# The reciprocal of the WKV denominator moved from VectorE to POOL, as a power of -1, with the rounds put in a new order

## The chip, the cores and the metric

The kernel runs on one core of one Trainium2 chip. The metric is the device time of that core in microseconds. One further execution was profiled; its trace is what the rows below come from.

## What is computed

An audio tower over `x` of shape (64, 256, 192). Pairs of time steps are merged by a softmax (leaving 64 sequences of 128 tokens), then come an RWKV time mix, a GELU MLP, a 12-head attention with normalised q and k, and a mixture of eight experts of which each token uses two. The change is in the time mix, whose core is a recurrence per channel:

```python
def step(carry, kv):
    p, q, o = carry
    kt, vt = kv
    no = jnp.maximum(o, u + kt)
    A = jnp.exp(o - no)
    Bc = jnp.exp(u + kt - no)
    y = (A * p + Bc * vt) / (A * q + Bc)
    ...
return jnp.einsum('btc,oc->bto', sr * y, Wo)      # sr = sigmoid(r)
```

The kernel divides numerator and denominator by `A`, so that with `z = exp(u + k - o)` the value is `y = (p + z v) / (q + z)`: one denominator and one numerator for each channel and token.

## The kernel before

The 64 sequences are worked in 16 groups of four (512 tokens). Tower work is staged over rounds: in round i the engines hold group i+1 (`gn`), i (`ga`), i-1 (`gb`), i-2 (`gc`), i-3 (`gr`) and i-4 (`gs`) at different stages. Stage A is the merge and the time mix, B the GELU MLP, C the attention, R the router. Each of the five engines has a `round_` of its own in which the steps stand in an order written out by hand; every engine works through its list strictly in that order, and a step waits with semaphores for what others must have done. Rounds 5 to 14 are one hardware loop, the others are unrolled. The experts follow after the last round, in a second pipeline that the change leaves alone.

The time mix of a group on VectorE (DVE), in the order of its dependences, with channels on 96 partitions and 1024 columns (two halves of the channels times 512 tokens): `a_mix` prepares the inputs of the r, k and v projections; `a_exponents` scans the running maximum `o_s` (L1253); `a_fraction_args` makes the argument of z; `a_scan_p` and `a_scan_q` scan p and q (L1283, L1287); `a_denominator` adds z and q into buffer wkv1 (L1292); `a_reciprocal` inverts that in place, in four quarters of 256 columns (L1301); `a_numerator` makes z v + p in wkv3 (L1296, L1297); `a_gate` multiplies by the gate (L1309) and then by the reciprocal, which gives `sy` (L1311). PE projects `sy` in `a_project` (L475), and `a_residual` takes the result (L1316). ScalarE (ACT) does the exponentials, POOL the small work on layer-norm statistics: `rstd` raises a variance plus eps to the power of -0.5 with `tensor_tensor(..., ALU.pow)` against the constant tile `neg_half` (L1089), on 4 columns, or on 8 for q and k. POOL also issues the eight indirect DMAs of `r_scatter` (L1126).

Beside the WKV steps DVE serves the attention of another group: `c_max` (L1356) for the maxima that ACT's `c_exps` wait for, `c_values` (L1365, L1366) for the scaled values that PE's `c_values` waits for, and `c_attn_add` (L1379), which ends that group's attention and which PE's `a_project` waits for too (semaphore `hF_ready`), since both use the same PSUM banks.

Of the kernel before, what the change touches and what calls it, by code (L numbers as in the profile page):

```python
# [14 lines left out]
P = 128  # L15
# [30 lines left out]
def build_tower(nc, a, out):  # L46
# [29 lines left out]
    with ExitStack() as ctx:  # L76
# [20 lines left out]
        neg_half = sg("neg_half", [P, 2 * G])  # L97
        lane8 = sg("lane8", [P, G, E])
# [130 lines left out]
        def ring(depth, name, shape, dt=F32):  # L229
# [25 lines left out]
            keep_arg keep_ready take_arg take_ready z_ready zexp_ready sy_ready  # L255
# [197 lines left out]
        def _(pe):  # L453
# [215 lines left out]
            def round_(i):  # L669
                gn, ga, gb, gc, gr, _ = stages(i)  # L670
                if gb is not None: b_mlp_up(gb, (4,))
                if gb is not None: b_mlp_up(gb, (5,))
                if ga is not None: a_hidden(ga)
                if gb is not None: b_mlp_down(gb, (0,))
                if gc is not None: c_keys(gc, gr)
                if gb is not None: b_mlp_down(gb, (1,))
                if gb is not None: b_mlp_down(gb, (2,))
                if ga is not None: a_r(ga)
                if gc is not None: c_queries(gc, 0)
                if gb is not None: b_mlp_down(gb, (3,))  # L680
                if ga is not None: a_k(ga)
                if gc is not None: c_scores(gc, 0, 0)
                if gc is not None: c_scores(gc, 0, 1)
                if gc is not None: c_queries(gc, 1, gb)
                if ga is not None: a_v(ga)
                if gc is not None: c_scores(gc, 1, 0)
                if gc is not None: c_scores(gc, 1, 1)
                if gc is not None: c_queries(gc, 2, gb)
                if gc is not None: c_values(gc, 0, gb)
                if gc is not None: c_scores(gc, 2, 0)  # L690
                if gc is not None: c_scores(gc, 2, 1)
                if gc is not None: c_queries(gc, 3, gb)
                if gc is not None: c_values(gc, 1, gb)
                if gc is not None: c_scores(gc, 3, 0)
                if gc is not None: c_project(gc, 0, ga)
                if gc is not None: c_scores(gc, 3, 1)
                if gb is not None: c_transposes(gb)
                if gc is not None: c_project(gc, 1, ga)
                if gc is not None: c_values(gc, 2, gb)
                if gb is not None: c_qkv(gb, (0,))  # L700
                if gb is not None: c_qkv(gb, (1,))
                if gc is not None: c_project(gc, 2, ga)
                if gc is not None: c_values(gc, 3, gb)
                if gc is not None: c_project(gc, 3, ga)
                if gb is not None: c_qkv(gb, (2,))
                if ga is not None: a_project(ga, gc)
                if gb is not None: c_qkv(gb, (3,))
                if gn is not None: a_delta(gn)
                if gc is not None: r_transposes(gc, gb)
                if gn is not None: a_scores(gn)  # L710
                if ga is not None: b_transposes(ga)
                if gc is not None: r_logits(gc)
                if ga is not None: b_mlp_up(ga, (0,))
                if ga is not None: b_mlp_up(ga, (1,))
                if gc is not None: r_places(gc)
                if ga is not None: b_mlp_up(ga, (2,))
                if ga is not None: b_mlp_up(ga, (3,))
# [75 lines left out]
        def _(act):  # L793
# [127 lines left out]
            def round_(i):  # L921
                gn, ga, gb, gc, _, _ = stages(i)
                if gc is not None: c_queries(gc, 0)
                if ga is not None: a_kv(ga, "k", k_s)
                if gc is not None: c_exps(gc, 0, 0)
                if gc is not None: c_queries(gc, 1)
                if gc is not None: c_exps(gc, 0, 1)
                if ga is not None: a_kv(ga, "v", v_c)
                if ga is not None: a_take_exp(ga)
                if ga is not None: a_keep_exp(ga)  # L930
# [3 lines left out]
                if ga is not None: a_z_exp(ga)  # L934
                if gc is not None: c_exps(gc, 2, 0)
                if gc is not None: c_queries(gc, 3)
                if gc is not None: c_values(gc, 0)
                if gc is not None: c_exps(gc, 2, 1)
                if gb is not None: ln_out(gb, "c", hnC, hC, rstdC, shiftC)
                if gc is not None: c_values(gc, 1)  # L940
                if gc is not None: c_exps(gc, 3, 0)
                if gb is not None: transposed(gb, "c", hTC, 4)
                if gc is not None: c_exps(gc, 3, 1)
                if gc is not None: c_values(gc, 2)
                if gb is not None: c_qkv(gb, 0)
                if gc is not None: c_values(gc, 3)
# [7 lines left out]
                if gn is not None: a_scores(gn)  # L954
                if ga is not None: transposed(ga, "b", hTB, 2)
                if gb is not None: c_k_norm(gb)
                if ga is not None: b_gelu(ga, 0)
                if ga is not None: b_gelu(ga, 1)
                if gb is not None: c_q_norm(gb)
                if ga is not None: b_gelu(ga, 2)  # L960
                if gc is not None: r_twice(gc)
                if ga is not None: b_gelu(ga, 3)
                if gn is not None: ln_out(gn, "a", hnA, hA, rstdA, shiftA)
                if ga is not None: b_gelu(ga, 4)
                if ga is not None: b_gelu(ga, 5)
                if gc is not None: r_gap(gc)
                if gn is not None: a_hidden(gn)
                if gb is not None: c_residual(gb)
                if gn is not None: a_gate(gn)
# [81 lines left out]
        def _(pool):  # L1051
            init = Chain(pool, S["p_init"], 11)
# [12 lines left out]
            init.link(nc.gpsimd.memset(neg_half[:, :], -0.5))  # L1065
            init.link(nc.gpsimd.iota(lane8_i[:, :, :], [[0, G], [1, E]], base=0, channel_multiplier=0))
# [13 lines left out]
            def rstd(g, name, out_, shift_, mv, n):  # L1080
# [13 lines left out]
                last.then_inc(S[f"{name}_rstd"], 1)  # L1094

# [77 lines left out]
        def _(dve):  # L1173
# [29 lines left out]
            wkv = Chain(dve, S["d_wkv"], 9)  # L1203
# [85 lines left out]
            def a_denominator(g):  # L1289
                wkv.begin(g, 4)  # L1290
                dve.wait_ge(S["zexp_ready"], g + 1)
                wkv.link(nc.vector.tensor_tensor(keep_flat, z_s, q_s[:, 0:M], ALU.add))  # L1292

            def a_numerator(g):
                wkv.begin(g, 6)
# [3 lines left out]
            def a_reciprocal(g, n):  # L1299
# [145 lines left out]
            def round_(i):  # L1445
                gn, ga, gb, gc, gr, _ = stages(i)
                if gr is not None: c_values(gr, 2)
                if gb is not None: a_reciprocal(gb, 1)
# [190 lines left out]
```

## Time and profile before

| | |
|---|---|
| time, median of 3 runs | 2093.18 us (2091.97 to 2100.26) |
| the profiled execution's own time | 2086.18 us |
| its span, first to last instruction | 2084.4 us |
| instructions | 32990 |
| a_denominator of group 0 and of group 15 begin at | 69.5 us and 1269.9 us |
| mean granted clock of TensorE, as a share of 2.4 GHz | 0.874 |

The span covers all but 1.8 us of the profiled execution. The sixteen groups with a time mix fill about its first 1300 us; three rounds without one follow, and from about 1460 us on the experts run.

### The profile page before, as it was taken

The page shows a single profiled execution, that of the slowest core. Times are in us where ns is not written, and L with a number is a line of the kernel's source. Part 1 is how long each engine was busy: PE and PEld are TensorE (multiplying, and loading weights), DVE is VectorE, ACT ScalarE, POOL GpSimd, SP SyncE. Part 2 cuts the span into 40 slices and gives each one's busy share as a digit, 9 for nine tenths or more (in the row PEclk, how much of TensorE's full clock was granted, in tenths as well). Part 3 has the DMA queues.
Part 4 walks back from the last instruction along what each step waited for, and adds up shares of the span by engine and source line. Part 5 has one row for each costly group of instructions (what it writes and reads, how often), then busy time and mean ns, then how long its engine had stood idle before and what let it go on. Part 6 is the DMA issues. An engine that isn't in the chain of part 4 may idle for free.

```text
span 2084.4 us, 32990 instructions
## 1 busy us (share of the span) xinstructions
PE 1776.7 (85%) x10605; PEld 1384.4 (66%) x10605; DVE 1471.4 (71%) x2705; ACT 1230.0 (59%) x3205; POOL 737.6 (35%) x756
## 2 busy tenths in 40 slices
PE   2478989889889889899898897874799999999992
PEld 1345666657657567566666675553699999999992
DVE  3566686776876866866868758232698998999981
ACT  1236766765775676667657656552666666666660
POOL 0001122221321231231222213222377777767772
PEclk9789889889789899798898797765899999999996
DMA  3000000010010010010000100043676767667655
GB/s 80 12 4 16 23 22 29 24 37 23 28 36 23 28 36 23 24 34 28 21 25 26 36 8 29 22 149 103 176 177 150 181 154 171 165 161 177 148 118 141
DMA packets 119429, 149.49 MB, mean 72 GB/s; under 512 B 16948, under 2 KB 100007, under 8 KB 119271
## 3 DMA queue, kind: packets, MB, share of 16 engines
q1 hardware_dynamic: 86944, 114.23, 18.1%
q0 software_dynamic: 28608, 32.66, 8.9%
q10 hardware_dynamic: 3814, 1.83, 0.4%
q8 instruction: 33, 0.54, 0.1%
q14 instruction: 30, 0.24, 0.0%
HBM read 100.14 MB, written 54.83 MB: 74 GB/s over the span
## 4 chain that ended last, share of the span: by engine, by line
PE 69%; DVE 14%; ACT 6%; issue 5%; DMA 2%; POOL 2%; SPq 0%; ACTq 0%; POOLq 0%; DVEq 0%
PE ps L762 11%; PE ps L535 8%; PE ps L775 8%; PE ps L543 6%; PE ps L466 6%; PE ps L627 5%; PE ps L458 4%; PE ps L777 4%; PE ps L611 3%; DVE nmax L1356 3%; PE ps L475 3%; PE ps L559 3%; PE ps L638 2%; ACT probs L900 2%; DVE q_s L1287 2%
## 5 line engine op out<-in xcount | busy, mean ns | idle before, releaser
L1158 POOL DMA_INDIRECT total<-ey,etoken x156 | 275.6, 1767 | 156.7 <-DMA total<-ey,etoken 65.3
L900 ACT ACTIVATE probs<-ps,nmax 128x128 f32<-128x128 f32 x768 | 271.6, 387 | 49.3 <-DVE nmax L1356 49.2
L775 PE MATMUL ps<-w_hl,h_hi 128*128 128x384 f32 x936 | 274.6, 364 | 3.8 <-DVE ey L1578 3.8
L1035 ACT ACTIVATE h_full<-ps,eb 128x512 f32<-128x512 f32 x234 | 167.7, 717 | 162.8 <-PE ps L762 162.7
L777 PE MATMUL ps<-w_hl,h_lo 128*128 128x192 f32 x936 | 235.6, 252 | 0.0
L627 PE MATMUL ps<-probs,vpad 128*32 128x128 f32 x1536 | 105.6, 377 | 100.0 <-DVE vpad L1366 94.7
L777 PEld LDWEIGHTS ps<-w_hl,h_lo 128*128 128x128 f32 x936 | 180.5, 193 | 0.0
L775 PEld LDWEIGHTS ps<-w_hl,h_hi 128*128 128x128 f32 x936 | 177.4, 190 | 4.5 <-issue 4.4
L535 PE MATMUL ps<-hTB,w_up 96*128 96x512 f32 x384 | 175.4, 609 | 2.5 <-ACT hTB L877 2.2
L900 ACT ACTIVATION_READ_ACCUMULATOR probs<-ps,nmax 128x1 f32 x768 | 174.1, 227 | 0.0
L1148 POOL TENSOR_TENSOR w_lo<-w_raw,w_hi 128x1536 fp32r<-128x1536 f32 x39 | 157.6, 4042 | 36.3 <-ACT w_hi L1016 36.3
L1036 ACT ACTIVATE h_hi<-ps,eb 128x512 fp32r<-128x512 f32 x234 | 169.1, 722 | 0.0
L611 PEld LDWEIGHTS ps<-qT,kT 32*128 32x128 f32 x1536 | 121.3, 262 | 69.7 <-ACT probs L900 31.5
L1087 POOL TENSOR_SCALAR shiftR<-mvR 128x4 f32<-128x4 f32 x16 | 3.7, 232 | 457.7 <-DVE mvR L1215 457.7
L611 PE MATMUL ps<-qT,kT 32*128 32x128 f32 x1536 | 144.9, 374 | 23.5 <-ACT probs L900 16.2
L1356 DVE TENSOR_REDUCE nmax<-ps 128x6 f32<-128x768 f32 x128 | 120.5, 953 | 58.7 <-PE ps L611 55.3
L1126 POOL DMA_INDIRECT expert_rows_in<-rowR,slot_i x128 | 145.1, 1134 | 43.5 <-issue 41.5
L627 PEld LDWEIGHTS ps<-probs,vpad 128*32 128x32 f32 x1536 | 75.2, 148 | 126.4 <-DVE vpad L1366 104.5
L1539 DVE TENSOR_TENSOR h_lo<-h_full,h_hi 128x512 fp32r<-128x512 f32 x234 | 147.9, 686 | 15.4 <-ACT h_hi L1036 14.8
L762 PE MATMUL ps<-x_hl,w_hi 128*128 128x512 f32 x468 | 146.7, 395 | 5.5 <-DVE x_hl L1546 5.5
L762 PE MATMUL ps<-x_hl,w_lo 128*128 128x512 f32 x468 | 145.1, 391 | 0.0
L543 PE MATMUL ps<-w_down,hid 128*128 128x192 f32 x768 | 134.2, 328 | 0.8 <-ACT hid L881 0.8
(227 smaller groups left out, 3945.4 us busy)
## 6 DMA issues: line engine op xcount, KB each, us to landing
w_raw<-in_L_ffn_w SPq DMA_DIRECT2D x39, 576.0 KB, 4.7
ex<-expert_rows_in SPq DMA_DIRECT2D x39, 528.0 KB, 5.1
w_raw<-in_L_ffn_w SPq DMA_DIRECT2D x39, 384.0 KB, 5.4
w_raw<-in_L_ffn_w SPq DMA_DIRECT2D x78, 192.0 KB, 5.7
xt<-in_x SPq DMA_DIRECT2D x16, 768.0 KB, 4.5
expert_rows_in<-xt SPq DMA_DIRECT2D x17, 528.0 KB, 7.4
total<-resC SPq DMA_DIRECT2D x16, 384.0 KB, 2.6
eb<-in_L_ffn_b SPq DMA_DIRECT2D x39, 96.0 KB, 3.6
```

What stands on the lines that cost most here:

```text
L535: last = nc.tensor.matmul(ps[:, 2 + m % 2, :], w_up[:, k, m * P:(m + 1) * P], hTB[:, k, :], start=(k == 0), stop=(k == KC - 1))
L543: last = nc.tensor.matmul(ps[:, 2 + t // 2, (t % 2) * C:(t % 2 + 1) * C], hid[:, m, t * T:(t + 1) * T], w_down[:, m, :], start=(m == 0), s ...
L611: last = nc.tensor.matmul(ps[:, 4 + j, heads], kT[rows, t, heads], qT[rows, t % 2, heads], start=True, stop=True)
L627: last = nc.tensor.matmul(ps[rows:rows + 32, 2, n // 4 * P:(n // 4 + 1) * P], vpad[:, t % 2, n, 32 * odd:32 * odd + 32], probs[:, t % 2, 2 ...
L762: last = nc.tensor.matmul(ps[:, m % 4, :], w, x, start=(n == 0), stop=(n == len(terms) - 1))
L775: nc.tensor.matmul(ps[:, 4 + s, 0:2 * C], h_hi[b][:, m, q], w2_hl[b][:, m, :], start=(m == 0), stop=False)
L777: last = nc.tensor.matmul(ps[:, 4 + s, 0:C], h_lo[b][:, m, q], w2_hl[b][:, m, 0:C], start=False, stop=(m == FM - 1))
L900: last = nc.scalar.activation(probs[:, t % 2, HJ * c + j, :], ps[:, 4 + j, c * P:(c + 1) * P], ACT.Exp, bias=nmax[:, t, j, c:c + 1], accum ...
L1035: nc.scalar.activation(h_full[:, m, :], ps[:, m % 4, :], ACT.Gelu, bias=eb1[u][:, m:m + 1])
L1036: nc.scalar.activation(h_hi[b][:, m, :], ps[:, m % 4, :], ACT.Gelu, bias=eb1[u][:, m:m + 1]).then_inc(S["e_hid"], 1)
L1158: nc.gpsimd.indirect_dma_start(total, bass.IndirectOffsetOnAxis(ap=etoken[u][:, s:s + 1], axis=0), ey[b][:, s, :], None, compute_op=ALU.ad ...
L1356: nc.vector.tensor_reduce(nmax[:, t, 2 * half:2 * half + 2, :], ps[:, 4 + 2 * half:6 + 2 * half, 0:HC * P] .rearrange("p j (c q) -> p j c ...
```

## The change

- `a_reciprocal` goes from DVE to POOL. It waits for a new semaphore `den_ready`, raises the denominator to the power of -1 with `tensor_tensor(..., ALU.pow)` against a constant column `neg_one` that is broadcast to 256 columns, in four quarters, and then signals `recip_ready`.
- `a_denominator` no longer waits for its own write; it signals `den_ready`. `a_numerator` needs no reciprocal ahead of it. `a_gate` does its first product and waits for `recip_ready` before its second.
- The `round_` lists of PE, ACT, POOL and DVE are written in a new order. Rounds are cut at another place, too: what was the start of a round's list is now partly the end of the one before, with the group names shifted to match (`gb` where `ga` was). Each group still takes the same number of rounds.
- The chains' counts follow (`wkv` 9 to 7, `init` 11 to 12).

```diff
+        neg_one = sg("neg_one", [P, 1])
...
+            init.link(nc.gpsimd.memset(neg_one[:, :], -1.0))
...
+            def a_reciprocal(g):
+                pool.wait_ge(S["den_ready"], g + 1)
+                stand_alone(pool)
+                q = KC * N // 4
+                for n in range(4):
+                    part = flat(1)[:, n * q:(n + 1) * q]
+                    last = nc.gpsimd.tensor_tensor(part, part, neg_one[0:CC, 0:1].to_broadcast([CC, q]), ALU.pow)
+                last.then_inc(S["recip_ready"], 1)
...
             def round_(i):
                 _, ga, gb, gc, gr, gs = stages(i)
-                if gs is not None: r_count(gs)
-                if gc is not None: rstd(gc, "c", rstdC[:, :], shiftC[:, :], mvC, G)
                 if gs is not None: r_scatter(gs)
+                if gb is not None: a_reciprocal(gb)
                 if gr is not None: rstd(gr, "r", rstdR[:, :], shiftR[:, :], mvR, G)
...
+                if gb is not None: rstd(gb, "c", rstdC[:, :], shiftC[:, :], mvC, G)
+                if gr is not None: r_count(gr)
...
-                wkv.link(nc.vector.tensor_tensor(keep_flat, z_s, q_s[:, 0:M], ALU.add))
+                nc.vector.tensor_tensor(keep_flat, z_s, q_s[:, 0:M], ALU.add).then_inc(S["den_ready"], 1)
...
-            def a_reciprocal(g, n):
-                q = M // 4
-                last = nc.vector.reciprocal(keep_flat[:, n * q:(n + 1) * q], keep_flat[:, n * q:(n + 1) * q])
-                if n == 3:
-                    wkv.begin(g, 5)
-                    wkv.link(last)
...
                 wkv.end()
+                dve.wait_ge(S["recip_ready"], g + 1)
                 nc.vector.tensor_tensor(sy[:, :], take, keep_flat, ALU.mult).then_inc(S["sy_ready"], 1)
```

What stands on DVE around the denominator, in the last unrolled round before the loop and on into the loop. The operand names are those of the program; wkv0 holds z, wkv1 the denominator, wkv2 and wkv3 the numerator; a name in brackets is the semaphore waited for. Before:

```order
L1292 TENSOR_TENSOR wkv1<-wkv0,q_s 96x1024 [waits zexp_ready]
L38 REGISTER_ALU
L1301 RECIPROCAL wkv1<-wkv1 96x256 [waits d_wkv]
L1355 ISA
L1356 TENSOR_REDUCE nmax<-ps 128x6 [waits scores_psum]
```

```order
L1301 RECIPROCAL wkv1<-wkv1 96x256
L1356 TENSOR_REDUCE nmax<-ps 128x6 [waits scores_psum]
L1301 RECIPROCAL wkv1<-wkv1 96x256 x2
L1365 RECIPROCAL rsums<-psums 128x12 [waits exp_ready,d_wkv]
L1366 TENSOR_TENSOR vpad<-v_s,rsums 128x12x16 [waits d_v]
L1296 TENSOR_TENSOR wkv3<-wkv0,v_c 96x1024
L1297 TENSOR_TENSOR wkv3<-wkv3,p_s 96x1024 [waits d_wkv]
L1309 SCALAR_TENSOR_TENSOR wkv2<-tanh_r,wkv3 96x1024 [waits tanh_r_ready,d_wkv]
L1311 TENSOR_TENSOR sy<-wkv2,wkv1 96x1024 [waits d_wkv]
L1379 TENSOR_TENSOR resC<-ps,resC 128x768 [waits res_ready,aproj_psum]
```

And after, on the same engine at the same place:

```order
L1304 TENSOR_TENSOR wkv1<-wkv0,q_s 96x1024 [waits zexp_ready,d_wkv]
L1361 REGISTER_ALU
L1362 TENSOR_REDUCE nmax<-ps 128x6 [waits scores_psum]
L1308 TENSOR_TENSOR wkv3<-wkv0,v_c 96x1024
L38 REGISTER_ALU
L1309 TENSOR_TENSOR wkv3<-wkv3,p_s 96x1024 [waits d_wkv]
```

```order
L1371 RECIPROCAL rsums<-psums 128x12 [waits exp_ready]
L1372 TENSOR_TENSOR vpad<-v_s,rsums 128x12x16 [waits d_v]
L1314 SCALAR_TENSOR_TENSOR wkv2<-tanh_r,wkv3 96x1024 [waits tanh_r_ready]
L38 REGISTER_ALU
L1317 TENSOR_TENSOR sy<-wkv2,wkv1 96x1024 [waits recip_ready,d_wkv]
L1385 TENSOR_TENSOR resC<-ps,resC 128x768 [waits res_ready,aproj_psum]
```

The four wide reciprocals are gone. Between the denominator and the product that gives `sy` stand one `c_max`, the two instructions of the numerator, one `c_values` and the gate's first product; the `c_max` and the `c_values` of one query tile that stood there before now stand ahead of the denominator.

POOL in the loop, before:

```order
L1126 DMA expert_rows_in<-rowR,slot_i 70144x264 [waits slots_ready,r_twice]
L1126 DMA expert_rows_in<-rowR,slot_i 70144x264 x7
L1087 TENSOR_SCALAR shiftR<-mvR 128x4 [waits r_stats]
L1088 TENSOR_SCALAR rstdR<-mvR 128x4
```

and after:

```order
L1137 DMA expert_rows_in<-rowR,slot_i 70144x264 [waits slots_ready,r_twice]
L1137 DMA expert_rows_in<-rowR,slot_i 70144x264 x7
L1104 TENSOR_TENSOR wkv1<-wkv1,neg_one 96x256 [waits den_ready]
L1104 TENSOR_TENSOR wkv1<-wkv1,neg_one 96x256 x3
L1087 REGISTER_ALU
L1089 TENSOR_SCALAR shiftR<-mvR 128x4 [waits r_stats]
```

The four powers stand between the scatter and the statistics of the router's layer norm, which need `c_attn_add` of the same round.

PE around `a_project`, after (before, the same steps stand there in the same order):

```order
L560 MATMUL ps<-w_qkv,hTC 128x384 [waits qkv_out]
L560 MATMUL ps<-w_qkv,hTC 128x384
L564 MATMUL ps<-w_qkv,hTC 128x192 x2
L476 MATMUL ps<-w_o,sy 128x192 [waits hF_ready,sy_ready]
L476 MATMUL ps<-w_o,sy 128x192 x7
```

Behind it stand the last tile of `c_qkv`, the transposes of the next group's input, of the router's and of the MLP's input, the whole MLP of the group, the keys and the next scores.

## Rows read from the trace of the kernel before

**Rows 1.** The page: busy time by engine, then the granted clock in 40 slices.
```profile
PE 1776.7 (85%) x10605; PEld 1384.4 (66%) x10605; DVE 1471.4 (71%) x2705; ACT 1230.0 (59%) x3205; POOL 737.6 (35%) x756
...
PEclk9789889889789899798898797765899999999996
```

**Rows 2.** The page, the chain that ended last, by engine.
```profile
PE 69%; DVE 14%; ACT 6%; issue 5%; DMA 2%; POOL 2%; SPq 0%; ACTq 0%; POOLq 0%; DVEq 0%
```

**Rows 3.** Busy time in three stretches: one round, then its PE half and score half.
```profile
core 0: us, PE busy (x) PEld busy (x) DVE busy (x) ACT busy (x) POOL busy (x), PEclk, DMA share, GB/s
598.00:680.00 82.00, 73.71 (x456) 52.28 (x455) 59.25 (x126) 53.72 (x166) 20.24 (x34) 0.85 0.08 28
340.00:360.00 20.00, 20.00 (x117) 14.47 (x116) 11.71 (x25) 7.26 (x12) 2.21 (x4) 1.00 0.00 0
360.00:380.00 20.00, 11.70 (x110) 7.69 (x108) 19.61 (x23) 18.54 (x83) 9.54 (x9) 0.76 0.15 55
```

**Rows 4.** DVE in order of time: start, duration, line, operation, count, idle before.
```profile
621.13 1.21 DVE L1292 TENSOR_TENSOR wkv<-wkv,q_s 96x1024 f32<-96x1024 f32 x1
622.37 1.75 DVE L1301 RECIPROCAL wkv<-wkv 96x256 f32<-96x256 f32 x1
624.82 0.96 DVE L1356 TENSOR_REDUCE nmax<-ps 128x6 f32<-128x768 f32 x1 [0.69 <-PE ps L611]
625.69 0.22 DVE L1365 RECIPROCAL rsums<-psums 128x12 f32<-128x12 f32 x1
625.94 0.36 DVE L1366 TENSOR_TENSOR vpad<-v_s,rsums 128x192 f32<-128x192 f32 x1
626.22 1.74 DVE L1301 RECIPROCAL wkv<-wkv 96x256 f32<-96x256 f32 x1
627.98 0.96 DVE L1356 TENSOR_REDUCE nmax<-ps 128x6 f32<-128x768 f32 x1
628.85 3.35 DVE L1301 RECIPROCAL wkv<-wkv 96x256 f32<-96x256 f32 x2
...
633.71 1.22 DVE L1296 TENSOR_TENSOR wkv<-wkv,v_c 96x1024 f32<-96x1024 f32 x1
...
637.47 1.22 DVE L1311 TENSOR_TENSOR sy<-wkv 96x1024 f32<-96x1024 f32 x1
640.37 0.96 DVE L1379 TENSOR_TENSOR resC<-ps,resC 128x768 f32<-128x768 f32 x1 [1.67 <-PE ps L638]
```

**Rows 5.** POOL by line and shape, 590 to 1290 us: count | busy, mean ns.
```profile
L1089 POOL TENSOR_TENSOR rstd_qk<-rstd_qk,neg_half 128x8 f32<-128x8 f32 x8 | 13.3, 1667 | 0.7
L1089 POOL TENSOR_TENSOR rstdB<-rstdB,neg_half 128x4 f32<-128x4 f32 x8 | 8.3, 1038 | 0.7
L1088 POOL TENSOR_SCALAR rstd_qk<-mv_qk 128x8 f32<-128x8 f32 x8 | 2.0, 247 | 0.5
L1088 POOL TENSOR_SCALAR rstdA<-mvA 128x4 f32<-128x4 f32 x8 | 1.8, 227 | 0.5
L1091 POOL TENSOR_TENSOR shiftA<-shiftA,rstdA 128x4 f32<-128x4 f32 x8 | 1.6, 200 | 0.6
```

**Rows 6.** The page, costliest groups: POOL's one wide elementwise instruction.
```profile
L1148 POOL TENSOR_TENSOR w_lo<-w_raw,w_hi 128x1536 fp32r<-128x1536 f32 x39 | 157.6, 4042 | 36.3 <-ACT w_hi L1016 36.3
```

**Rows 7.** The denominators, all sixteen: min/median/max ns, first and last start.
```profile
L1292 DVE TENSOR_TENSOR wkv<-wkv,q_s x16: 1211/1213/1222, 69.5 to 1269.9; 96x1024 f32<-96x1024 f32 x16
```

**Rows 8.** PE in order of time, around a_project of one round.
```profile
641.46 0.81 PE L563 MATMUL ps<-w_qkv,hTC 97*128 97x192 f32 x4
642.11 2.76 PE L475 MATMUL ps<-w_o,sy 96*128 96x192 f32 x16
644.71 1.46 PE L559 MATMUL ps<-w_qkv,hTC 97*128 97x384 f32 x4
646.01 0.81 PE L563 MATMUL ps<-w_qkv,hTC 97*128 97x192 f32 x4
```

**Rows 9.** PE in order of time, a_project of group 0.
```profile
82.46 5.04 PE L475 MATMUL ps<-w_o,sy 96*128 96x192 f32 x16 [21.76 <-DVE sy L1311]
```

**Rows 10.** Busy time and granted clock in short stretches around it; columns as in Rows 3.
```profile
62.00:64.00 2.00, 0.00 (x0) 0.00 (x0) 1.97 (x5) 1.93 (x3) 0.00 (x0) 0.76 0.00 0
64.00:66.00 2.00, 0.00 (x0) 0.00 (x0) 1.97 (x2) 0.98 (x1) 0.00 (x0) 0.50 0.00 0
84.00:86.00 2.00, 2.00 (x8) 2.00 (x7) 0.00 (x0) 0.00 (x0) 0.00 (x0) 0.50 0.00 0
86.00:88.00 2.00, 1.50 (x7) 1.21 (x5) 0.46 (x1) 0.00 (x0) 0.00 (x0) 0.77 0.00 0
642.00:644.00 2.00, 2.00 (x14) 2.00 (x13) 0.87 (x6) 0.71 (x2) 0.64 (x3) 1.00 0.61 197
```

More of the change, by code:

```diff
@@ L254, in build_tower @@
             tanh_r_ready k_ready v_ready
-            keep_arg keep_ready take_arg take_ready z_ready zexp_ready sy_ready
+            den_ready recip_ready keep_arg keep_ready take_arg take_ready z_ready zexp_ready sy_ready
             oproj_psum hB_ready
@@ L669, in round_ @@
             def round_(i):
-                gn, ga, gb, gc, gr, _ = stages(i)
+                _, ga, gb, gc, gr, _ = stages(i)
+                if gb is not None: a_hidden(gb)
+                if gc is not None: b_mlp_down(gc, (0,))
+                if gc is not None: b_mlp_down(gc, (1,))
+                if gc is not None: b_mlp_down(gc, (2,))
+                if gr is not None: c_scores(gr, 0, 0)
+                if gc is not None: b_mlp_down(gc, (3,))
+                if gb is not None: a_r(gb)
@@ new lines, in round_ @@
+                if gr is not None: c_scores(gr, 0, 1)
+                if gr is not None: c_queries(gr, 1, gc)
+                if gb is not None: a_k(gb)
+                if gr is not None: c_scores(gr, 1, 0)
+                if gr is not None: c_scores(gr, 1, 1)
+                if gr is not None: c_queries(gr, 2, gc)
+                if gb is not None: a_v(gb)
+                if gr is not None: c_values(gr, 0, gc)
+                if gr is not None: c_scores(gr, 2, 0)
+                if gr is not None: c_scores(gr, 2, 1)
@@ new lines, in round_ @@
+                if gr is not None: c_queries(gr, 3, gc)
+                if gr is not None: c_values(gr, 1, gc)
+                if gr is not None: c_scores(gr, 3, 0)
+                if gr is not None: c_project(gr, 0, gb)
+                if gr is not None: c_scores(gr, 3, 1)
+                if gr is not None: c_project(gr, 1, gb)
+                if gr is not None: c_values(gr, 2, gc)
+                if gc is not None: c_transposes(gc)
+                if gc is not None: c_qkv(gc, (0,))
+                if gr is not None: c_project(gr, 2, gb)
@@ new lines, in round_ @@
+                if gr is not None: c_values(gr, 3, gc)
+                if gc is not None: c_qkv(gc, (1,))
+                if gr is not None: c_project(gr, 3, gb)
+                if gc is not None: c_qkv(gc, (2,))
+                if gb is not None: a_project(gb, gr)
+                if gc is not None: c_qkv(gc, (3,))
+                if ga is not None: a_delta(ga)
+                if gr is not None: r_transposes(gr, gc)
+                if ga is not None: a_scores(ga)
+                if gb is not None: b_transposes(gb)
@@ L671, in round_ @@
+                if gr is not None: r_logits(gr)
+                if gb is not None: b_mlp_up(gb, (0,))
+                if gr is not None: r_places(gr)
+                if gb is not None: b_mlp_up(gb, (1,))
+                if gc is not None: c_keys(gc, gr)
+                if gb is not None: b_mlp_up(gb, (2,))
+                if gb is not None: b_mlp_up(gb, (3,))
                 if gb is not None: b_mlp_up(gb, (4,))
                 if gb is not None: b_mlp_up(gb, (5,))
-                if ga is not None: a_hidden(ga)
@@ L684, in round_ @@
[L684 to L713, printed above, removed]
@@ L933, in round_ @@
                 if gc is not None: c_exps(gc, 1, 1)
-                if ga is not None: a_z_exp(ga)
+                if ga is not None: a_kv(ga, "v", v_c)
+                if ga is not None: a_take_exp(ga)
                 if gc is not None: c_exps(gc, 2, 0)
@@ L937, in round_ @@
                 if gc is not None: c_values(gc, 0)
+                if ga is not None: a_keep_exp(ga)
                 if gc is not None: c_exps(gc, 2, 1)
[L939 removed]
                 if gc is not None: c_values(gc, 1)
+                if ga is not None: a_z_exp(ga)
                 if gc is not None: c_exps(gc, 3, 0)
@@ L944, in round_ @@
                 if gc is not None: c_values(gc, 2)
+                if gc is not None: c_values(gc, 3)
                 if gb is not None: c_qkv(gb, 0)
-                if gc is not None: c_values(gc, 3)
                 if gb is not None: c_qkv(gb, 1)
```

103 lines of the change are left out of this document (42 added, 61 removed).

## Prediction, written before the changed kernel ran

> **What bounds the kernel now.** I read the page's busy shares and the chain first. PE is busy 85% of the span, DVE 71%, ACT 59%, POOL 35% [rows 1], and the chain that ended last lies 69% on PE and 14% on DVE [rows 2]. These are averages, so the next view is busy time by stretch [rows 3]. A round lasts 80.0 us on average: the sixteen denominators begin from 69.5 to 1269.9 us, and (1269.9 - 69.5) / 15 = 80.0 [rows 7]. Within a round there are two halves. In one (340 to 360 us) PE is busy all 20 us and DVE 11.7. In the other, where scores are made and the WKV chain runs, DVE is busy 19.6 of 20 us and ACT 18.5, PE only 11.7, and the granted clock is 0.76. The four wide reciprocals of a group lie in this second half, on the engine that bounds it. POOL is busy 20 us of a round of 82.
>
> The third view is DVE in order of time in that half [rows 4]. The reader is to see one interval: the denominator is done at 621.13 + 1.21 = 622.34 us, and the product that gives `sy` begins at 637.47, so 15.1 us later. In it lie the four reciprocals (1.75 + 1.74 + 3.35 = 6.84 us), two maxima, two `c_values`, the numerator and the gate's first product. This interval is what the change replaces. `c_attn_add` and PE's `a_project` stand right behind it.
>
> **The new operation.** The trace has no power over 256 columns, but it has the same operation of the same engine on 4 and on 8 columns: 1038 and 1667 ns [rows 5]. The difference is 629 ns for 4 columns, so 157 ns per column and a fixed part of 1038 - 4 x 157 = 409 ns. That a power is dear by the column, not only by the instruction, is the one fact that decides this case: a plain add to a scalar on the same columns goes from 227 to 247 ns, 5 ns per column, thirty times less [rows 5]. A quarter of the reciprocal then takes 0.41 + 256 x 0.157 = 40.7 us, and the four 162.7 us. The 96 partitions in place of 128 I count at no gain.
>
> The bounds. Low: short instructions may show a worse rate than long ones. The wide subtraction takes 4042 / 1536 = 2.63 ns per column [rows 6], against the 5.0 of the short ones, a factor of 0.53. With that factor on the power's 157 ns, a quarter takes 0.41 + 256 x 0.083 = 21.6 us, the four 86.3. High: if the fixed part is only that of a plain instruction (200 ns, [rows 5]), a column of the 8 costs (1667 - 200) / 8 = 183 ns, a quarter 47.1 us, the four 188. I take 162.7, since 4 and 8 columns are one instruction with one input doubled, while the factor of 0.53 is borrowed from operations whose loop does almost nothing per column.
>
> **What lies beside it.** Call the four powers together R. From the end of the denominator DVE has, by the new order, one maximum (0.96), the numerator (2 x 1.22), `c_values` (0.22 + 0.36) and the gate's first product (1.22): 5.2 us [rows 4]. Then it stands at `recip_ready`. Queued behind that wait on DVE are `c_attn_add`, the residual, all statistics of the round, the router's choice and the next group's mixing. For these wait: PE, which can still do the last values, projections and three tiles of `c_qkv`, and then stands at `a_project` for `sy` and for `hF_ready`; ACT at `r_out`; and on POOL the four small power chains, which stand behind the reciprocal and which nobody can ask for sooner. Before, PE did that same work within the 15.1 us, so nothing of size is left to lie beside 162.7 us. Nor can one group's stall hide another's: each group's next steps stand in the same lists behind the wait.
>
> **The sum for one group.** Interval from denominator to `sy`: from 15.1 to R. The `c_max` and `c_values` that now stand ahead of the denominator: 0.69 + 0.96 + 0.22 + 0.36 = 2.2 us more on the rest of the round. PE comes late to `a_project` now: it begins at 642.11 us [rows 8], though `sy` is there at 638.7; with PE waiting it would begin after `sy` and a `c_attn_add` of 0.96 plus the signals, at about 639.8, so 2.3 us are given back. The clock: after 20 idle us PE's granted clock is 0.50, which is the level of 1.2 GHz, and it is still 0.50 over 84 to 86 us with PE busy throughout, 0.77 over the next two [rows 10]; `a_project` took 5.04 us there [rows 9] and 2.76 us in the round at 642 us [rows 8], where the clock is 1.00, or 2.4 GHz. That is 2.3 us more, and the same ratio of 1.83 on the `c_qkv` tile behind it (1.46 + 0.81 = 2.27 us, [rows 8]) another 1.9. Together: R - 15.1 + 2.2 - 2.3 + 2.3 + 1.9 = R - 11.0. With R = 162.7 that is 151.7 us a group, and 16 groups give 2427 us.
>
> The rest of the new order I count at nothing. It moves the r, k and v projections, the keys and the maxima against each other inside the two halves of a round; PE's work and ACT's are the same instructions, and with PE idle for over 140 us of each round what it might win or lose is a microsecond or two per round, some 30 us in all, which the bounds of R cover many times. The three rounds without a time mix and the experts (from 1460 us on) have no such power in them. The extra memset of one column costs nothing. The profiled execution's time is 2086.2 us, so 2086 + 2427 = 4513; the median of the runs shown lies 7 us above the profiled one, which is nothing here. I forecast **4510 us**.
>
> With the bounds of R: 16 x (86.3 - 11.0) = 1205 gives 3291 us, and 16 x (188 - 11.0) = 2832 gives 4918 us.
>
> **A rule of the skill against the row.** The Trainium skill, GPSIMD Engine Reference, sections "Performance versus the Vector engine" and "Engine selection", puts GPSIMD at about 2.6 cycles per element of a two-input elementwise instruction, roughly twice the vector engine's time, and calls it the wrong place for elementwise work; it names no price for a power. The wide subtraction agrees with it (2.63 ns per column, [rows 6]); the power's 157 ns does not. By the page's rate the change would be the first rival below, an estimate of some 2030 us.
>
> **Rival 1, a cheap power (faster).** The cost of 4 and 8 columns is that of entering a slow routine, and over 256 columns the power runs like the wide subtraction: 0.20 + 256 x 0.00263 = 0.87 us a quarter, R = 3.5 us. It is then hidden beside DVE's 5.2 us. DVE's second half of the round loses 6.8 us, but PE comes 3.4 us late to `a_project` already (642.1 against 638.7), so about half is gained: 16 x 3.5 = 56 us, 2030 us. For it: the reciprocals lie on the bounding engine [rows 3]. Against it: 629 ns for four further columns cannot be an entry cost. It decides at R = 11.0 us, or 2.75 us a quarter, (2.75 - 0.41) / 256 = 9 ns per column; above that the change loses. A sentence of the Trainium skill, Advanced Engine Details and Errata, says that GPSIMD's and VectorE's instructions interfere at a shared port; with it the numerator could not lie beside the power, and this rival would shrink toward no change. No row here shows it.
>
> **Rival 2, a power that runs at a better rate over long rows (slower, by less).** R = 86.3 as above, 3291 us. For it: POOL's plain instructions do just that. Against it: their short rows are nearly all fixed cost.
>
> **Rival 3, in between.** A routine that overlaps many columns, R from 11 to 86 us: 2090 to 3290 us. No row speaks for it.
>
> That the change does not do what it says is out: by the order the four powers stand on POOL, and no reciprocal of 96x256 is left on DVE.
>
> **How the numbers follow.** The linear price (R from 140 to 180, 4150 to 4790 us) has 0.64, a better rate down to rival 2's bound 0.14, up to the high bound 0.05; rival 3 has 0.05 and the cheap power 0.12. The range takes in the first three, 0.83: 3290 to 4920 us. A measurement of this kernel can tell about 0.5% from no change. Faster by more than that: 0.11, nearly all of rival 1. Within it: 0.01. Slower: 0.88.
>
> **What would show it.** In the changed profile, the power on 96x256 should read 40.7 us (20 to 47 by the bounds) x64, POOL some 2600 us busier, DVE idle about 157 us before each L1317 and released by POOL, PE idle nearly as long before `a_project`, which should take about 5 us at a granted clock of 0.50, and the denominators about 232 us apart. The sum is wrong if a quarter takes under 20 us; the step that failed is then the price per column. If the quarters read 41 us but the denominators stand much closer than 232 us, something does lie beside the stall.

## The result and the profile after

The changed kernel takes 4560.02 us (median of 4 runs, 4558.93 to 4565.18) against 2094.55 us for the kernel before on the same occasion: a ratio of 2.177, 95% interval 2.172 to 2.182. Forecast was 4510 us, with a range of 3290 to 4920.

The page of the changed kernel: busy shares, the busy tenths of PE and POOL and the clock in 40 slices, the chain that ended last, and the two costliest waits. Compare with [rows 1] and [rows 2].

```profile
PE 1808.7 (40%) x10605; PEld 1399.6 (31%) x10605; DVE 1369.6 (30%) x2641; ACT 1226.6 (27%) x3205; POOL 3380.2 (74%) x821
...
PE   1040606060606050514142332324141507699996
...
POOL 4959495959595959596968687887879692277775
PEclk7575757575757575757565666666575756699998
...
POOL 50%; PE 28%; issue 12%; DVE 7%; ACT 2%; DMA 0%; ACTq 0%; another core or an unknown queue 0%; SPq 0%; DVEq 0%; POOLq 0%
...
L1104 POOL TENSOR_TENSOR wkv<-wkv,neg_one 96x256 f32<-96x256 f32 x64 | 2632.3, 41144 | 217.2 <-DVE wkv L1304 217.2
L476 PE MATMUL ps<-w_o,sy 96*128 96x192 f32 x256 | 86.1, 529 | 2485.5 <-DVE resC L1385 2146.9
...
L1317 DVE TENSOR_TENSOR sy<-wkv 96x1024 f32<-96x1024 f32 x16 | 19.5, 1222 | 2514.5 <-POOL wkv L1104 2514.5
```

POOL was 35% busy and is the engine of half the chain now. The power over 256 columns takes 41.1 us, 64 times: 2632 us, more than the whole kernel took before. DVE waits 2514.5 us for it in 16 waits, ahead of the product that gives `sy`, and PE stands nearly as long ahead of `a_project`. PE's busy time hardly changed (1777 to 1809 us); over the sixteen stalls its tenths swing between 0 and 6, and the clock between 7 and 5. The sixteen denominators, to be held against [rows 7]:

```profile
L1304 DVE TENSOR_TENSOR wkv<-wkv,q_s x16: 1220/1221/1223, 69.6 to 3585.9; 96x1024 f32<-96x1024 f32 x16
```

They stand (3585.9 - 69.6) / 15 = 234.4 us apart, where it was 80.0. One stall in order of time, first DVE and then PE (start, duration, line, operation, idle before). It answers to [rows 4] and [rows 8]; the denominator rows are those of the next group, the rest of this one:

```profile
1634.91 1.22 DVE L1317 TENSOR_TENSOR sy<-wkv 96x1024 f32<-96x1024 f32 x1 [156.41 <-POOL wkv L1104]
1636.06 0.95 DVE L1385 TENSOR_TENSOR resC<-ps,resC 128x768 f32<-128x768 f32 x1
...
1704.42 1.22 DVE L1304 TENSOR_TENSOR wkv<-wkv,q_s 96x1024 f32<-96x1024 f32 x1
1705.57 0.95 DVE L1362 TENSOR_REDUCE nmax<-ps 128x6 f32<-128x768 f32 x1
1706.43 1.21 DVE L1308 TENSOR_TENSOR wkv<-wkv,v_c 96x1024 f32<-96x1024 f32 x1
1707.68 1.22 DVE L1309 TENSOR_TENSOR wkv<-wkv,p_s 96x1024 f32<-96x1024 f32 x1
1712.23 0.23 DVE L1371 RECIPROCAL rsums<-psums 128x12 f32<-128x12 f32 x1 [3.34 <-ACT probs L901]
```

```profile
1482.93 0.81 PE L564 MATMUL ps<-w_qkv,hTC 97*128 97x192 f32 x4
1637.15 5.46 PE L476 MATMUL ps<-w_o,sy 96*128 96x192 f32 x16 [153.40 <-DVE resC L1385]
1642.40 2.27 PE L560 MATMUL ps<-w_qkv,hTC 97*128 97x384 f32 x4
1644.51 0.82 PE L564 MATMUL ps<-w_qkv,hTC 97*128 97x192 f32 x4
```

DVE does what it can beside the power (the rows from 1705.57 on) and then idles 156 us. PE idles 153 us, is released by `c_attn_add` (L1385) 1.0 us after `sy`, and runs `a_project` in 5.46 us where it took 2.76. Its granted clock in that stretch:

```profile
1640.00:1642.00 2.00, 2.00 (x8) 2.00 (x7) 0.00 (x0) 1.07 (x3) 1.16 (x4) 0.50 0.00 0
...
1644.00:1646.00 2.00, 2.00 (x14) 1.61 (x13) 1.16 (x7) 0.64 (x2) 0.35 (x2) 0.99 0.00 0
```

### The profile page after: what moved, and what is told of

It is laid out like the page before. It is cut to its first block, busy times and chain, and to the rows that moved or that the text cites. A ratio compares the mean times of both kernels' runs of the same rounds, so it can differ in the third digit from the quotient of the medians.

```text
span 4557.9 us, 32949 instructions
## 1 busy us (share of the span) xinstructions
PE 1808.7 (40%) x10605; PEld 1399.6 (31%) x10605; DVE 1369.6 (30%) x2641; ACT 1226.6 (27%) x3205; POOL 3380.2 (74%) x821
## 4 chain that ended last, share of the span: by engine, by line
POOL 50%; PE 28%; issue 12%; DVE 7%; ACT 2%; DMA 0%; ACTq 0%; another core or an unknown queue 0%; SPq 0%; DVEq 0%; POOLq 0%
POOL wkv L1104 49%; PE ps L763 5%; PE ps L776 4%; PE ps L536 3%; PE ps L476 3%; PE ps L544 3%; PE ps L778 2%; PE ps L612 2%; PE ps L459 1%; PE ps L467 1%; DVE nmax L1362 1%; PE ps L628 1%; DVE q_s L1299 1%; ACT probs L901 1%; PE ps L649 1%
## 5 line engine op out<-in xcount | busy, mean ns | idle before, releaser
L1104 POOL TENSOR_TENSOR wkv<-wkv,neg_one 96x256 f32<-96x256 f32 x64 | 2632.3, 41144 | 217.2 <-DVE wkv L1304 217.2
L476 PE MATMUL ps<-w_o,sy 96*128 96x192 f32 x256 | 86.1, 529 | 2485.5 <-DVE resC L1385 2146.9
L476 PEld LDWEIGHTS ps<-w_o,sy 96*128 96x128 f32 x256 | 78.9, 331 | 2490.4 <-DVE sy L1317 2490.4
L1317 DVE TENSOR_TENSOR sy<-wkv 96x1024 f32<-96x1024 f32 x16 | 19.5, 1222 | 2514.5 <-POOL wkv L1104 2514.5
L800 ACT ACTIVATE rowR<-resC,shiftR,rstdR 128x192 f32<-128x192 f32 x64 | 29.8, 535 | 2198.2 <-POOL shiftR L1093 2198.2
L1089 POOL TENSOR_SCALAR shiftC<-mvC 128x4 f32<-128x4 f32 x16 | 10.8, 676 | 274.1 <-DVE mvC L1227 274.1
L1036 ACT ACTIVATE h_full<-ps,eb 128x512 f32<-128x512 f32 x234 | 167.7, 716 | 164.7 <-PE ps L763 164.5
L1137 POOL DMA_INDIRECT expert_rows_in<-rowR,slot_i x128 | 154.3, 1206 | 52.3 <-issue 50.0
L901 ACT ACTIVATION_READ_ACCUMULATOR probs<-ps,nmax 128x1 f32 x768 | 164.5, 214 | 0.0
```

The costliest lines, as they stand in the source:

```text
L476: last = nc.tensor.matmul(o, xT[:, k * N + t * T:k * N + (t + 1) * T], w[:, k, :], start=(k == 0), stop=(k == KC - 1))
L901: last = nc.scalar.activation(probs[:, t % 2, HJ * c + j, :], ps[:, 4 + j, c * P:(c + 1) * P], ACT.Exp, bias=nmax[:, t, j, c:c + 1], accum ...
L1036: nc.scalar.activation(h_full[:, m, :], ps[:, m % 4, :], ACT.Gelu, bias=eb1[u][:, m:m + 1])
L1104: last = nc.gpsimd.tensor_tensor(part, part, neg_one[0:CC, 0:1].to_broadcast([CC, q]), ALU.pow)
```

## Experiments

Two things are open after the result. The whole loss is said to be the length of one operation, the power; that its price is linear, and that the loss follows it, can be tested. And the change has two parts, the hand-over and the new order, of which the trace shows only the sum. The medians of the kernel before differ by up to 0.5% between the occasions (2085 to 2095 us), so each kernel is compared by its ratio to the runs of the kernel before made with it.

### The price of the power by its length

```diff
-                q = KC * N // 4
-                for n in range(4):
-                    part = flat(1)[:, n * q:(n + 1) * q]
+                for at, q in ((0, 64), (64, 128), (192, 320), (512, 512)):
+                    part = flat(1)[:, at:at + q]
```

> The changed kernel with the 1024 columns of the power cut into 64, 128, 320 and 512 in place of four times 256. Theory (a fixed part and a price per column, here 0.41 us and 159 ns by the 41.1 us of a quarter): 10.6, 20.8, 51.3 and 81.8 us, the total time that of the changed kernel. Rival (the rate improves with the row's length and is only just reached): the piece of 512 under 78 us, that of 64 over 11.5 us.

One execution, 4560.64 us. POOL's groups by shape, count | busy, mean ns of one:

```profile
L1103 POOL TENSOR_TENSOR wkv<-wkv,neg_one 96x512 f32<-96x512 f32 x16 | 1310.5, 81907 | 0.0
L1103 POOL TENSOR_TENSOR wkv<-wkv,neg_one 96x320 f32<-96x320 f32 x16 | 820.9, 51307 | 0.0
L1103 POOL TENSOR_TENSOR wkv<-wkv,neg_one 96x128 f32<-96x128 f32 x16 | 331.5, 20717 | 0.0
...
L1103 POOL TENSOR_TENSOR wkv<-wkv,neg_one 96x64 f32<-96x64 f32 x16 | 170.5, 10658 | 218.6 <-DVE wkv L1303 218.6
```

From 64 to 512 columns the slope is (81907 - 10658) / 448 = 159.0 ns per column. The price that 4 and 8 columns gave (157) holds up to 512 columns; a longer row earns nothing. How the 1024 columns are cut does not matter: the four together are 164.6 us, as four quarters are.

### One quarter on POOL, three on VectorE

```diff
-                for n in range(4):                       # POOL
+                for n in range(1):
...
+            def a_reciprocal(g):                         # DVE, behind the c_max that follows the denominator
...
+                for n in range(1, 4):
+                    part = keep_flat[:, n * q:(n + 1) * q]
+                    last = nc.vector.reciprocal(part, part)
+                last.then_inc(S["recip_ready"], 1)
```

> The changed kernel, with one quarter of the reciprocal as a power on POOL (R = 41.1 us) and three quarters on VectorE beside it. Theory (above the break-even every microsecond of R costs a microsecond a group): the changed kernel lost (4560 - 2094) / 16 = 154.1 us a group at R = 164.4, so R - 10.3; at 41.1 that is 30.8 us a group, 2587 us (2560 to 2600). Rival (something else stood in the long stall, such as the cold clock, and goes with it, or a shorter stall overlaps more of the other work): under 2540 us.

2567.75 us against 2085.44, ratio 1.232 (1.230 to 1.234). The quarter on POOL (R is the time of all powers of a group, here of one):

```profile
L1104 POOL TENSOR_TENSOR wkv<-wkv,neg_one 96x256 f32<-96x256 f32 x16 | 658.5, 41156 | 214.4 <-DVE wkv L1304 214.4
```

That is (2567.75 - 2085.44) / 16 = 30.1 us a group with R = 41.2 us, where the changed kernel lost (4560.02 - 2094.55) / 16 = 154.1 at 164.6. Between the two a microsecond of R costs (154.1 - 30.1) / (164.6 - 41.2) = 1.005 us a group. The theory stands: between these two lengths the stall is paid in full, and no part of it found cover that a shorter one would not have. Drawn back to zero loss the line puts the break-even at R = 41.2 - 30.1 / 1.005 = 11.2 us. That is drawn far beyond the two points, and no run lies there.

### Only the hand-over, in the old order

```diff
+                if gb is not None: a_reciprocal(gb)      # POOL, before's order, behind r_scatter
...
-                if gb is not None: a_reciprocal(gb, 1)   # and the other three calls on DVE
```

> The kernel before with its own order of the rounds, and only the reciprocal moved to POOL as a power of -1. Theory: with R = 164.4 us for the four powers and the interval from denominator to sy of 15.1 us before, 16 x (164.4 - 15.1) = 2389 us more, plus 4.2 us a group for the cold clock and less 2.3 for PE's lateness (30 us): about 4505 us, some 50 us less than the changed kernel, since the c_max and c_values are not ahead of the denominator. Rival (the new order makes room for the stall): over 4600 us.

4508.81 us, ratio 2.154 (2.151 to 2.158). It came out as expected: the new order makes the changed kernel 51 us slower than it need be, 3.2 us a group (the kernel with four lengths, run on this occasion with the new order, took 4560.64). Between `sy` and the next denominator stand seven `c_max` and three `c_values` in the new order, six and two in the old, which is the pair that the prediction priced at 2.2 us. The traces put the time elsewhere than at that pair alone, though. From the mixing (L1248) to the scan (L1265), first in the changed kernel and then in this one:

```profile
1667.67 1.22 DVE L1248 TENSOR_TENSOR wkv<-hTA 96x1024 f32<-96x1024 f32 x1 [5.50 <-ACT hTA L850]
1687.92 2.28 DVE L1265 TENSOR_TENSOR_SCAN o_s<-decay,k_s 96x1024 f32<-96x1024 f32 x1
```

```profile
1653.26 1.21 DVE L1248 TENSOR_TENSOR wkv<-hTA 96x1024 f32<-96x1024 f32 x1
1668.05 2.28 DVE L1265 TENSOR_TENSOR_SCAN o_s<-decay,k_s 96x1024 f32<-96x1024 f32 x1
```

It is 20.3 us in place of 14.8, 5.5 more; the new order has more maxima in this stretch, and DVE waits 3.9 us for the scores ahead of one of them. The stretches before and after it are about 1 us shorter each (32.8 in place of 33.8, and 16.5 in place of 17.5), which leaves 3.4 in this round. So the 3.2 us are shown as a sum, and which step of the new order makes them is not.

### Only the new order

```diff
+            def a_reciprocal(g):                         # DVE in place of POOL
+                dve.wait_ge(S["den_ready"], g + 1)
+                q = M // 4
+                for n in range(4):
+                    part = keep_flat[:, n * q:(n + 1) * q]
+                    last = nc.vector.reciprocal(part, part)
+                last.then_inc(S["recip_ready"], 1)
...
+                if gb is not None: a_reciprocal(gb)
                 if gb is not None: a_numerator(gb)
                 if gr is not None: c_values(gr, 3)
```

> The new order of all rounds is kept, but the four reciprocals run on VectorE again, right behind the maximum that follows the denominator. This splits the change into its two parts. Theory (the loss is the power's own duration, the order is worth a microsecond or two per round): 2060 to 2130 us, so within 2% of the kernel before. Rival (the new order itself loses, for instance through the c_max and c_values that now stand ahead of the denominator, 2.2 us a group, or gains): outside that, over 2130 or under 2060 us.

2133.32 us against 2093.47, ratio 1.022 (1.017 to 1.027): just above the theory's upper end, so on the rival's side. With the reciprocal back on DVE the new order loses 2.2%. PE in order of time in one round shows where:

```profile
648.92 0.92 PE L639 MATMUL ps<-w_ao,oT 128*128 128x192 f32 x4 [0.18 <-ACT oT L909]
652.64 1.92 PE L628 MATMUL ps<-probs,vpad 128*32 128x128 f32 x24 [2.80 <-DVE vpad L1379]
654.49 2.93 PE L560 MATMUL ps<-w_qkv,hTC 97*128 97x384 f32 x4
657.21 1.49 PE L564 MATMUL ps<-w_qkv,hTC 97*128 97x192 f32 x4
```

The last `c_values` stands on DVE behind all four quarters and the numerator. PE waits 2.8 us for it, and after that wait works at the lower clock: the granted clock (third column from the end) is 1.00 over 646 to 650 us and 0.50 over 654 to 658.

```profile
646.00:650.00 4.00, 3.13 (x12) 2.01 (x12) 4.00 (x4) 2.87 (x15) 0.00 (x0) 1.00 0.00 0
654.00:658.00 4.00, 4.00 (x13) 2.41 (x10) 0.97 (x1) 1.02 (x4) 0.00 (x0) 0.50 0.00 0
```

The first three groups of matmuls from there (652.64 to 657.21) take 1.92, 2.93 and 1.49 us, where the kernel with the numerator on POOL (below), whose clock stays at 1.00 there, takes 1.07, 1.56 and 0.81: 2.9 us more, on top of the wait itself. In this run the clock is 0.50 to 0.63 in every round over the 3 us that begin 13.3 us behind the denominator's start. It is not shown to be the wait's doing, however: in two of the ten rounds from the fourth to the thirteenth PE waited only 0.4 us, and the matmuls ahead of the wait were slow already (the same group of 2.93 us at 563.59 and 898.17 us, with a granted clock of 0.50 over 560 to 564 and 566 to 570):

```profile
569.50 1.92 PE L628 MATMUL ps<-probs,vpad 128*32 128x128 f32 x24 [0.42 <-DVE vpad L1379]
```

With the last `c_values` in this place, the new order has no room ahead of it for both the reciprocal and the numerator on DVE.

### A cheap operation in the power's place

```diff
-Z_CAP = 60.0
+Z_CAP = 1.0
...
-                    ... neg_one[0:CC, 0:1].to_broadcast([CC, q]), ALU.pow)
+                    ... neg_one[0:CC, 0:1].to_broadcast([CC, q]), ALU.mult)
```

> The changed kernel with a multiplication by -1 in place of the power on POOL, and the cap on the argument of z lowered from 60 to 1 so that values stay finite: the reciprocal is left out, everything else runs. It measures what the new order and the hand-over would give with a POOL operation at the price of a plain one. Theory, by the sum's terms: four instructions of about 0.87 us, hidden beside VectorE's 5.2 us, 2030 us (2000 to 2060). Rival (contention or the new order take the gain): 2080 us or more.

This kernel leaves the reciprocal out, so its output is not the function's; it only measures time. The cap on the argument of z is lowered with it, so that values stay finite.

2047.27 us, ratio 0.978 (0.977 to 0.980): a gain of 46 us, where the first rival was worked out at 56. So the new order would have paid with a POOL operation at the price of a plain one; the change failed by the price of one operation, not by its plan. DVE, POOL and PE in one round:

```profile
602.15 1.22 DVE L1304 TENSOR_TENSOR wkv<-wkv,q_s 96x1024 f32<-96x1024 f32 x1
603.29 0.95 DVE L1362 TENSOR_REDUCE nmax<-ps 128x6 f32<-128x768 f32 x1
604.16 1.65 DVE L1308 TENSOR_TENSOR wkv<-wkv,v_c 96x1024 f32<-96x1024 f32 x1
605.85 1.52 DVE L1309 TENSOR_TENSOR wkv<-wkv,p_s 96x1024 f32<-96x1024 f32 x1
609.78 0.23 DVE L1371 RECIPROCAL rsums<-psums 128x12 f32<-128x12 f32 x1 [2.42 <-ACT probs L901]
```

```profile
L1104 POOL TENSOR_TENSOR wkv<-wkv,neg_one x64: 603/1506/1590, 71.4 to 1235.0; 96x256 f32<-96x256 f32 x64
```

```profile
616.62 2.76 PE L476 MATMUL ps<-w_o,sy 96*128 96x192 f32 x16
```

The products of the numerator, 1.21 and 1.22 us beside the power, take 1.65 and 1.52 beside a product on POOL, and a POOL quarter takes from 603 to 1590 ns. That is 0.7 us more on DVE, but DVE then idles 2.42 us for ACT's exponentials, so in this round the delay costs nothing. The missing gain is elsewhere: from the denominator to `a_project` it is 616.62 - 602.15 = 14.5 us, where it was 642.11 - 621.13 = 21.0, so 6.5 less; but the denominators stand (1230.9 - 70.0) / 15 = 77.4 us apart in place of 80.0. The rest of the round is 3.9 us longer, about what the new order cost in the stalled kernel.

### The reciprocal on VectorE, the last c_values ahead of its last quarter

Against the run at 1.022:

```diff
-                if gb is not None: a_reciprocal(gb)
-                if gb is not None: a_numerator(gb)
+                if gb is not None: a_reciprocal(gb, (0, 1, 2))
                 if gr is not None: c_values(gr, 3)
+                if gb is not None: a_reciprocal(gb, (3,))
+                if gb is not None: a_numerator(gb)
```

> The new order with the reciprocal on VectorE as in the run of 2133 us, but c_values of the last query tile moved ahead of the last quarter and of the numerator. Theory (the new order loses there because the last c_values stands behind 6.6 us of reciprocals and 2.4 us of numerator while ACT has long been done, and c_attn_add then waits 4.5 us for PE): 4.2 to 4.5 us a group back, 2061 to 2066 us, faster than the kernel before. Rival (VectorE's own length sets the round): 2115 us or more.

2072.48 us against 2085.44, ratio 0.994 (0.993 to 0.995). From 1.022 that is 2.8%, some 58 us or 3.6 us a group, of the 4.2 to 4.5 expected; the time lies above the expected 2061 to 2066 us and far below the rival's 2115. In one round PE now waits 1.14 us for DVE ahead of `a_project` (at 636.08 us), which it did not do before. That the place of the last `c_values` made the 2.2% is thereby shown, and the new order with a plain VectorE reciprocal is a little faster than the kernel before.

### The division of labour turned round

POOL does the numerator, two cheap instructions; VectorE keeps the reciprocal.

```diff
+            def a_numerator(g):                          # POOL, in the place of a_reciprocal
+                pool.wait_ge(S["den_ready"], g + 1)
...
+                nums.begin(g)
+                nums.link(nc.gpsimd.tensor_tensor(flat(3), flat(0), v_c[:, :], ALU.mult))
+                nums.end()
+                nc.gpsimd.tensor_tensor(flat(3), flat(3), p_s[:, 0:KC * N], ALU.add).then_inc(S["num_ready"], 1)
...
-                if gb is not None: a_numerator(gb)       # DVE
+                if gb is not None: a_reciprocal(gb)
```

> The division of labour turned round, in the new order: VectorE does the reciprocal (6.6 us), POOL the two instructions of the numerator (about 2.9 us each), since a product is cheap there; c_values of the last tile stands behind the four quarters. Theory: 2.4 us a group less on VectorE than in the run of 2133 us, of which nearly all stands ahead of the last c_values: 2133 - 16 x 2.4 = 2095 us. Rival (the two engines slow each other at their memory port, as 1.21 us products took 1.65 us beside POOL's product): 2110 us or more.

2048.62 us, ratio 0.983 (0.981 to 0.984). Neither theory: the gain over the run at 1.022 is 3.9%, 5.1 us a group and not 2.4. PE in one round, and its clock:

```profile
614.04 1.07 PE L628 MATMUL ps<-probs,vpad 128*32 128x128 f32 x24
```

```profile
614.00:618.00 4.00, 4.00 (x38) 3.16 (x38) 2.40 (x3) 1.73 (x6) 0.00 (x0) 1.00 0.00 0
```

With DVE's list 2.4 us shorter ahead of the last `c_values`, PE comes to it without a wait, the clock is 1.00, and the three groups of matmuls take the 2.9 us less that were named above. The two together are 5.3 us. From the third round on the clock in this place is 1.00 in every round.

Both edits together, numerator on POOL and the last `c_values` ahead of the last quarter:

> Both: numerator on POOL, reciprocal on VectorE, c_values of the last tile ahead of the last quarter. Theory: PE, ACT and VectorE then have nearly the work of the run with the cheap operation (2047 us) plus what the reciprocal puts on VectorE: 2045 to 2065 us. Rival (contention): 2080 us or more.

2046.92 us, ratio 0.981 (0.980 to 0.983); the lower end of the expectation. The same kernel once more:

> The kernel of the ratio 0.9814 once more, on the same chip as the one beside it, to compare the two orders directly. Theory: 0.98 again (0.979 to 0.984).

2057.47 us against 2093.08, ratio 0.982 (0.981 to 0.984). This is the version to keep: 1.8 to 1.9% faster than the kernel before, and as fast as the kernel with the reciprocal left out (0.978) to within 0.4%. The kernel with the numerator on POOL alone (0.983, 0.981 to 0.984) can't be told from it: once POOL has the numerator, no run shows a gain from moving `c_values`. Part of the gain is clock: the mean granted clock of the profiled executions is 0.892 and 0.896, where it is 0.874 before. DVE in one round, then POOL:

```profile
688.35 4.96 DVE L1312 RECIPROCAL wkv<-wkv 96x256 f32<-96x256 f32 x3
693.40 0.23 DVE L1377 RECIPROCAL rsums<-psums 128x12 f32<-128x12 f32 x1
...
693.94 1.74 DVE L1312 RECIPROCAL wkv<-wkv 96x256 f32<-96x256 f32 x1
```

```profile
687.75 2.34 POOL L1104 TENSOR_TENSOR wkv<-wkv,v_c 96x1024 f32<-96x1024 f32 x1 [10.68 <-DVE wkv L1305]
690.17 2.34 POOL L1106 TENSOR_TENSOR wkv<-wkv,p_s 96x1024 f32<-96x1024 f32 x1
```

POOL is done with both after 4.8 us, beside DVE's 6.7 us of reciprocals, and no quarter is longer than before.

### Is the new order needed for that?

The same POOL numerator in the kernel before, its order unchanged.

> The kernel before in its own order, with only the numerator moved to POOL, where it starts with the denominator's end and takes 2 x 2.34 us beside VectorE's 6.8 us of reciprocals. Theory (the gain of the turned-round division is VectorE's 2.44 us a group, whatever the order): 16 x 2.4 = 39 us less than the kernel before, a ratio of 0.981. Rival (in the old order PE comes to a_project late anyway and takes the gain, so the new order is needed for it): a ratio over 0.99.

2084.16 us against 2093.08, ratio 0.996 (0.994 to 0.997). The rival holds: most of the gain needs the new order. PE and DVE in one round:

```profile
627.15 1.22 DVE L1319 TENSOR_TENSOR sy<-wkv 96x1024 f32<-96x1024 f32 x1
632.35 0.96 DVE L1387 TENSOR_TENSOR resC<-ps,resC 128x768 f32<-128x768 f32 x1 [3.98 <-PE ps L638]
```

```profile
634.10 2.76 PE L475 MATMUL ps<-w_o,sy 96*128 96x192 f32 x16
```

`sy` is ready at 628.4 us, and its product begins 12.8 us after the denominator's end in place of 15.1, but PE comes to `a_project` 5.7 us later, where in [rows 8] it came 3.4 us late. DVE's saving turned into PE's lateness. One `vpad` is held up beside POOL there (last section), but PE uses it only at 623.20 us, 3.7 us after it is ready, so that is not the reason.

## Why the prediction was right

**The price per column.** 157 ns by the difference of two short rows; 159 measured, and R 164.6 us in place of 162.7. Two lengths of the same instruction were enough to price a third 32 times as long; both borrowed bounds (83 and 183 ns) were far off. The time was missed by 50 us: the 1.9 us a group make 30 of them, 8 are the median of the kernel before (2094.55) against the profiled 2086.2 that the sum started from, 3 are rounding, and the other terms make the rest.

**What lies beside the stall.** Nothing but the 5.2 us named. DVE's idle time before `sy` is 2514.5 / 16 = 157 us a group, as forecast, and the slope of 1.005 between a quarter and the whole shows that the stall is bare beyond the first 41 us. The step said PE would still do three tiles of `c_qkv` and then stand; the rows at 1482.93 and 1637.15 us show it.

**The terms of the sum.** PE starts `a_project` 1.0 us after `sy` (1.1 forecast). The cold clock: from `a_project` to the transposes behind it 1645.16 - 1637.15 = 8.0 us, where it was 646.66 - 642.11 = 4.55: 3.5 us, forecast 4.2. Of that, `a_project` is 2.7 longer (2.3 forecast) and the `c_qkv` tile behind it 0.8 (1.9 forecast), since the clock is back at 0.99 over 1644 to 1646 us. The round without R is 234.4 - 164.6 = 69.8 us, by the sum 80.0 - 11.0 = 69.0.

**The term that was mis-sized.** "The rest of the new order I count at nothing", beside its 2.2 us. Measured between the two orders it is 3.2 us a group, so 1.0 was missed, 16 us in all; the clock's term, 0.7 too high, took 11 of them back, and that is luck. With what was measured the sum is 164.7 (the denominator's end to `sy`) - 15.1 + 3.2 - 2.4 + 3.5 = 153.9 us a group, against 154.1. The sentence held for the stalled kernel only: with the reciprocal on VectorE the new order is worth 2.2% to the wrong side, and 0.6% to the right one once `c_values` is moved. Both are under 3% of the change, and they decide everything once the stall is gone.

**The rivals.** The cheap power would have given 2047 us (worked out: 2030). Its direction was right. Its sum took half of DVE's 6.8 us as gained and left out the new order's own cost; measured, 6.5 us are gained up to `a_project` and 3.9 lost in the rest of the round. The contention, of which the prediction says that the numerator could then not lie beside POOL's work, is there, but the numerator lies beside it all the same, 0.7 us longer and at no cost in the round shown. The sentence of the Trainium skill that the prediction took for it, Advanced Engine Details and Errata, section "Mode Summary", speaks of VectorE's two-port (2p) instructions only; no run here shows in which mode these products run. The break-even is 11.2 us where the line through two runs is drawn back to zero, 11.0 forecast; no run tests it, and at R = 4.3 us, where the line would give a gain of 6.9 us a group, the cheap operation gained 2.9. The lower rate over long rows and the case in between are out by the run with four lengths.

## What to carry to other kernels

Price an operation by the element, from two lengths of the same instruction in the trace at hand, before it is moved to an engine that looks idle: an engine 35% busy was no place for work at 159 ns per column, though it was one for work at 2.3. When an engine is to be relieved, hand over what is cheap on the other one: here the numerator (2.3 ns per column on POOL), and keep what only the first does well (6.7 ns for the reciprocal on VectorE). And an order of work is tuned to the length of what stands in it: price the order apart from the operation, since the same order was 2.2% slower or 1.7% faster by whether two instructions of the numerator stood in one gap.

## What the runs showed of the hardware

A power on POOL costs 159 ns per column over 96 partitions, from 64 to 512 columns, beside a fixed part of about 0.4 to 0.5 us, and 157 over 128 partitions and 4 to 8 columns; a product costs 2.3 ns (2.34 us for 1024 columns).

A product of two SBUF operands on DVE and one on POOL hold each other up. Beside POOL's cheap product, DVE's took 1.65 in place of 1.21 us. In the old order with POOL's numerator, a DVE product of 0.36 us ran into it:

```profile
617.93 1.57 DVE L1374 TENSOR_TENSOR vpad<-v_s,rsums 128x192 f32<-128x192 f32 x1
```

```profile
616.94 2.35 POOL L1104 TENSOR_TENSOR wkv<-wkv,p_s 96x1024 f32<-96x1024 f32 x1
```

It ended at 619.50 us, just behind POOL's instruction (619.29). Reciprocals, which have one input, took 1.70 us in the kernel with POOL's numerator as in the one without it. Beside the power, DVE's products kept their 1.21 us. The Trainium skill, GPSIMD Engine Reference, section "Specifications", names contention with DVE instructions that have two SBUF inputs; the 1.57 us agree with that. Not every POOL instruction does it: the products beside the power were undisturbed.

A pause of PE of 2.8 us, with the granted clock at 1.00 before it, was followed by 0.50, and the matmuls behind it took 2.9 us more than at 1.00. Another round of the same run had the clock at 0.50 ahead of the same place already, and a pause of only 0.42 us, so no run shows that the pause brings the clock down.
